# Attention on one Trainium2 core: four probability blocks of a chunk joined by three chained accumulating DMAs, row sums in two TensorE passes

## What is computed

```python
qkv = jnp.einsum('bnd,ed->bne', x, w_qkv)
q, k, v = jnp.split(qkv, 3, axis=-1)          # each to 16 heads of 32
dots = jnp.einsum('bhnd,bhmd->bhnm', q, k) * SCALE
attn = jax.nn.softmax(dots, axis=-1)
out = jnp.einsum('bhnm,bhmd->bhnd', attn, v)
```

## Time and profile before

| | us |
|---|---|
| median of three runs | 1830.68 |
| profiled execution, span from the first to the last instruction | 1825.5 |
| what lies between the two | 5.2 |
| busy: TensorE matmul | 1787.7 (98%) |
| busy: VectorE | 1455.1 (80%) |
| busy: ScalarE | 1448.1 (79%) |
| busy: POOL | 182.8 (10%) |
| VectorE adds into dve_sum, line 896, x320 of 2306 ns | 737.8 |
| DMA queue of POOL, share of 16 engines | 19.8% |

### The profile page before, as it was taken

One profiled execution on the slowest core, in us unless ns is written; L12 is line 12 of the kernel. 1 busy time (PEld: TensorE's weight loads), 2 busy tenths in 40 slices (PEclk: granted clock), 3 DMA queues, 4 the chain that ended last, 5 costly groups with the idle time before them and its releaser, 6 DMA issues. The chain is left out here.

```text
span 1825.5 us, 40458 instructions
## 1 busy us (share of the span) xinstructions
PE 1787.7 (98%) x16186; PEld 906.5 (50%) x16186; DVE 1455.1 (80%) x1582; ACT 1448.1 (79%) x1581; POOL 182.8 (10%) x158
## 2 busy tenths in 40 slices
PE   9999998999999999999999999999989999999997
PEld 7887885333333333333333333333336776644443
DVE  5444346889899898898998989989984778788898
ACT  5344357999999999999999999999965555556487
POOL 0000000010010010010010010100113221000044
PEclk9999999999999999999999999999999999999998
DMA  8665555436446346355464463464456440122075
GB/s 300 216 226 205 206 201 180 105 87 166 96 99 170 93 101 166 82 134 133 94 142 124 94 164 91 108 160 96 102 140 215 139 138 24 64 127 127 1 295 206
DMA packets 106370, 256.32 MB, mean 140 GB/s; under 512 B 8180, under 2 KB 24692, under 8 KB 96756
## 3 DMA queue, kind: packets, MB, share of 16 engines
q1 hardware_dynamic: 97012, 187.08, 28.5%
q0 software_dynamic: 9216, 67.11, 19.8%
HBM read 105.01 MB, written 82.05 MB: 102 GB/s over the span
## 5 line engine op out<-in xcount | busy, mean ns | idle before, releaser
L896 DVE TENSOR_TENSOR dve_sum<-dve_sum,probs 128x2048 f32<-128x2048 f32 x320 | 737.8, 2306 | 13.1 <-ACT probs L817 3.3
L817 ACT ACTIVATE probs<-score_others,shift_now 128x1536 f32<-128x1536 f32 x384 | 597.5, 1556 | 0.0
L984 PE MATMUL mixed_ps<-probs,value_piece 128*32 128x512 f32 (+1 forms) x3840 | 407.9, 515 | 1.2 <-ACT probs L817 0.2
L816 ACT ACTIVATE probs<-score_first,shift_now 128x512 f32<-128x512 f32 x384 | 266.5, 694 | 4.1 <-PE score_others L951 1.1
L951 PE MATMUL score_first<-first_queries,key_piece 32*128 32x512 f32 x768 | 245.4, 424 | 4.6 <-ACT probs L816 3.0
L951 PE MATMUL score_others<-first_queries,key_piece 32*128 32x512 f32 x2304 | 247.8, 425 | 0.0
L951 PE MATMUL score_others<-q_second,key_piece 32*128 32x512 f32 x2304 | 247.3, 424 | 0.0
L951 PE MATMUL score_first<-q_second,key_piece 32*128 32x512 f32 x768 | 245.1, 424 | 0.1
L951 PEld LDWEIGHTS score_first<-q_second,key_piece 32*128 32x128 f32 x768 | 122.0, 183 | 183.6 <-ACT probs L816 100.8
L951 PEld LDWEIGHTS score_first<-first_queries,key_piece 32*128 32x128 f32 x768 | 121.8, 183 | 183.2 <-ACT probs L816 84.3
L817 ACT ACTIVATE probs_paired<-score_others,shift_now 128x1536 f32<-128x1536 f32 x128 | 198.2, 1548 | 0.0
(11 more groups left out here) (252 smaller groups left out, 2596.7 us busy)
## 6 DMA issues: line engine op xcount, KB each, us to landing
probs_paired<-probs_paired POOLq DMA_DIRECT2D x64, 1024.0 KB, 8.0
o_scratch<-out_parts SPq DMA_DIRECT2D x33, 512.0 KB, 2.8
k_scratch<-parts SPq DMA_DIRECT2D x32, 512.0 KB, 4.9
q_scratch<-parts SPq DMA_DIRECT2D x32, 512.0 KB, 2.7
key_piece<-k_scratch SPq DMA_DIRECT2D x32, 512.0 KB, 5.2
h_scratch<-h SPq DMA_DIRECT2D x5, 2816.0 KB, 8.1
h<-h_scratch SPq DMA_DIRECT2D x5, 2816.0 KB, 11.4
v_scratch<-values SPq DMA_DIRECT2D x32, 256.0 KB, 2.0
```

Of the source, the lines that this page charges most:

```text
L816: nc.scalar.activation(block_probs(k)[:, 0:CH], score_first[:], ACT.Exp, bias=shift[:, c:c + 1], scale=SCALE).then_inc(probs_done, 1)
L817: nc.scalar.activation(block_probs(k)[:, CH:HPG * CH], score_others[n % 2][:], ACT.Exp, bias=shift[:, c:c + 1], scale=SCALE).then_inc(prob ...
L896: nc.vector.tensor_tensor(total[:], first[:], block_probs(k)[:], ALU.add).then_inc(dve_added, 1)
L984: last = nc.tensor.matmul(mixed_ps[j * HD:(j + 1) * HD, lo:hi], v_group[k // KPP][:, k % KPP, j * HD:(j + 1) * HD], block_probs(k)[:, j * ...
```

## The change

PAIRS becomes (2, 3) and (4, 5). Each pair's DMA waits for the values of its first block and the exponentials of its second, no longer for the values of the second. When both have landed, POOL issues a third DMA that adds the tile of blocks 2 and 3 to that of blocks 4 and 5. Two sum passes are left: one in step 0 from the joined tile, one in step 1 from dve_sum. VectorE adds the blocks 0, 1 and 6 to 15. ScalarE's waits for the four tiles are new: block 2 for the third DMA of the chunk before (four_landed, which POOL passes on), blocks 3 and 5 for its pair DMAs (pairs_landed), block 4 for the sums. Singles still share six tiles.

```diff
-    PAIRS = ((4, 5), (9, 10))
-    TO_SUMS = (0, 1)
+    PAIRS = ((2, 3), (4, 5))
     ADD_ORDER = [k for k in range(KB) if not any(k in pair for pair in PAIRS)]
 
-    SUMS_AT = ((0,), (1, 2))
+    SUM_PARTS = 2
+    SUMS_AT = ((0,), (1,))
...
-                            if i in TO_SUMS:
+                            if i is not None and k == PAIRS[i][1]:
+                                act.wait_ge(pairs_landed, it * CPB + c + 1)
+                            elif i == 0:
+                                act.wait_ge(four_landed, it * CPB + c + 1)
+                            elif i == 1:
                                 act.wait_ge(sums_done, it * CPB + c + 2)
-                            elif i is not None:
-                                act.wait_ge(dve_added, (it * CPB + c) * ADDS + added_at(PAIRS[i][0]))
...
-                            if pair_of(k) is None:
-                                v.wait_ge(probs_done, (it + 1) * EXPS + (c * KB + k + 1) * 2)
-                            else:
-                                v.wait_ge(joined[pair_of(k)], 16 * (it * CPB + c + 1))
+                            v.wait_ge(probs_done, (it + 1) * EXPS + (c * KB + k + 1) * 2)
...
+                pool.sem_inc(pairs_landed, 1)
+                pool.sem_inc(four_landed, 1)
                 pool.wait_ge(w_in, 16)
                 with pool.Fori(0, ITERS) as it:
                     for c in range(CPB):
                         for i, pair in enumerate(PAIRS):
 
-                            pool.wait_ge(mixed_done, (it + 1) * BLOCKS + c * KB + pair[1] + 1)
+                            pool.wait_ge(mixed_done, (it + 1) * BLOCKS + c * KB + pair[0] + 1)
+                            pool.wait_ge(probs_done, (it + 1) * EXPS + (c * KB + pair[1] + 1) * 2)
                             pool.sem_inc(may_join, 1)
-                            nc.gpsimd.dma_start(probs_paired[i][0][:], probs_paired[i][1][:], accum_op=ALU.add).then_inc(joined[i], 16)
+                            nc.gpsimd.dma_start(probs_paired[i][0][:], probs_paired[i][1][:], accum_op=ALU.add).then_inc(pair_joined, 16)
+                        pool.wait_ge(pair_joined, 16 * len(PAIRS) * (it * CPB + c + 1))
+                        pool.sem_inc(pairs_landed, 1)
+                        nc.gpsimd.dma_start(probs_paired[1][0][:], probs_paired[0][0][:], accum_op=ALU.add).then_inc(four_joined, 16)
                         if c == W_AT:
...
-                for signal in joined:
-                    pool.wait_ge(signal, 16 * ITERS * CPB)
+                        pool.wait_ge(four_joined, 16 * (it * CPB + c + 1))
+                        pool.sem_inc(four_landed, 1)
...
-                    if at < len(TO_SUMS):
-                        part = probs_paired[TO_SUMS[at]][0]
-                        pe.wait_ge(joined[TO_SUMS[at]], 16 * f)
+                    if at == 0:
+                        part = probs_paired[1][0]
+                        pe.wait_ge(four_joined, 16 * f)
                     else:
                         part = dve_sum[(f + 1) % 2]
                         pe.wait_ge(dve_added, (f + 1) * ADDS)
```

More of the change, by code:

```diff
@@ L698, in attend @@
         dve_added, may_join = sem("dve_added"), sem("may_join")
-        joined = [sem(f"joined{i}") for i in range(len(PAIRS))]
+        pair_joined, four_joined = sem("pair_joined"), sem("four_joined")
+        pairs_landed, four_landed = sem("pairs_landed"), sem("four_landed")
         mixed_copied = sem("mixed_copied")
@@ L971, in sums @@
                         last = nc.tensor.matmul(mixed_ps[j * HD:(j + 1) * HD, :], keep.ones[:, 0:HD], part[:, j * CH:(j + 1) * CH],
-                                                start=at == 0, stop=at == len(TO_SUMS))
-                    if at == len(TO_SUMS):
+                                                start=at == 0, stop=at == SUM_PARTS - 1)
+                    if at == SUM_PARTS - 1:
                         last.then_inc(sums_done, 1)
@@ L1015, in first_product @@
                                          start=m == 0, stop=m == len(terms) - 1)
-                for at in range(len(TO_SUMS) + 1):
+                for at in range(SUM_PARTS):
                     sums(CHUNKS, at)
```

## The result

The changed kernel takes 1863.43 us, the median of four runs (1861.02 to 1866.18), against 1830.84 us before: a ratio of 1.0174, with a 95% interval of 1.0155 to 1.0193. It is slower by 32.6 us. (A ratio and its interval are estimated from the fast runs of both kernels, and can differ by up to 0.002 from the quotient of the two medians.) The forecast was 8 us faster, and the range ended at 1843.

The account below looks back on a forecast made before the run. TensorE was taken to lead, with 1.3 us of ScalarE's slack. Span 1825.5 - 19 (removed pass) + 11 (late chain in seven loading chunks) = 1817.5; from the median, 1830.7 - 8 = 1822.5 us, range 1810 to 1843.

Parts of the forecast that it names:

- the signs that it set for being wrong: Quiet chunks waiting for the DMA, seven loading chunks below 33 or above 37 us, or last-values copy late behind VectorE's adds.
- What bounds the kernel: Attention chunks of 33.2 us: TensorE's contiguous steps add up to 33.1 us and lead, with 1.3 us of ScalarE's slack behind.
- The removed pass: Step 1, one sum pass fewer: 0.6 us a chunk gained, 0.3 turned into a wait for VectorE; 19 us over 32 chunks.
- VectorE's stop before block 6: VectorE's adds in each chunk: 0.4 to 0.5 us idle before block 6, covered by 0.4 us spare, costed at nothing.
- Rival C: VectorE becomes the bound: its last add comes 0.3 us later, quiet gain 10 us, chain loses 8, about 1829 us; chance 0.17.
- The quiet chain: Three DMAs in chunks without loads: landing at 624.6, needed by 626.5, 2 us to spare; 24 or 25 chunks keep 0.6.
- Rival A: The three-DMA chain is on time everywhere, in loading chunks too: 1811.5 us; chance 0.22.
- The loading chain: Three DMAs in seven chunks that fetch keys and values: landed at 562.3, needed at 560.2, 2.1 us late.
- The loss per late chunk: Step 0 after a loading chunk: 2.1 us late, 0.4 comes back, loss 1.6 us x 7 = 11 us.
- The last chunk: End of attention: other loads in it and no next chunk to hold up, so no lateness counted.
- rival B: Step 0 after the loading chunks: chain late by much more, 4.4 x 7 = 31 us lost, 1842.5 us; chance 0.28.
- The rule against the trace: GpSimd-issued 1 MB DMA: the skill's fit gives 4.4 us, the trace 6.9 to 10.5; by the fit the chain is never late.

Follow-up runs that it names:

- less_pass: The kernel before with the second of its three sum passes left out, DMAs, loads and waits as before: 1814.92 us, ratio 0.9908.
- stall_half_filled: The changed kernel with 18 idle matmuls ahead of step 0's wait for the third DMA in the chunks after loads: 1849.47 us, ratio 1.0110.
- nothing_beside_end: The changed kernel, loading chunks fetching only the first keys early, other loads and store after the third DMA; last chunk's output and token loads also held: 1897.32 us.
- third_skipped: The changed kernel with the third DMA adding only 128 of 2048 columns in the fourth chunk of each iteration: 1816.72 us, ratio 0.9922.
- keys_ahead3: The changed kernel, loading chunks fetching first and second keys ahead of the DMA chain, first values beside it, the rest and the store after: 1841.80 us, ratio 1.0055.
- loads_after: The changed kernel, loading chunks storing early and issuing the second to fourth load pieces only after the third DMA has landed: 1857.71 us, ratio 1.0138.

## Why the prediction was wrong

Point by point, by its own steps. Of the signs that it set for being wrong two came: the seven chunks took above 37 us (38.27 to 39.05), and four quiet chunks show the wait for the chain, though of 1.08 us at most. Two slips in its sums are small: 2.1 less 0.4 is 1.7 and not 1.6, and 1830.7 - 8 is 1822.7.

*What bounds the kernel*, right: TensorE leads, with ScalarE close behind, and less_pass shows it.

*The removed pass*, right in kind, 0.52 us a chunk for 0.6. The waits for dve_sum and for the last values stayed small, and VectorE's stop before block 6 is there and covered, as costed:

```profile
680.88 20.90 DVE L896 TENSOR_TENSOR dve_sum<-dve_sum,probs 128x2048 f32<-128x2048 f32 x9 [0.52 <-ACT probs L820]
702.18 0.69 DVE L831 COPY mixed<-mixed_ps 128x512 f32<-128x512 f32 x1 [0.40 <-PE mixed_ps L990]
```

VectorE idles 0.52 us ahead of block 6, where 0.4 to 0.5 was foreseen, and still waits 0.40 us for the last values, which is the spare that was worked out. Rival C is out.

*The quiet chain*, right in that it costs almost nothing, wrong in its size: the third DMA is issued 14.05 us after the first in the chunk at 614.79 (12.7 to 14.3 in all 24), for 12.5 predicted, since a second DMA behind the first lands 6.5 us after it (3.8 + 9.7 - 7.0) and not 5.0. The 5.0 was meant as the later of two bounds, and the measured landing lies beyond it. Of the 2 us of spare next to nothing was left: hence the four short waits. Rival A, the chain in time everywhere, is out by that alone.

*The loading chain* is the step that failed, and in it one term: "5.0 + 1.1 for the second behind it". By that the second lands 6.1 us behind the first and 14.2 us after the first is issued; measured were 8.2 to 9.6 us and 16.6 to 17.9 (17.5 in the chunk at 680.13, 3.9 + 13.6). About half of the miss, 1.5 us, is not the loads at all: it is the 6.5 for 5.0 that quiet chunks show too. The other half is that the loads delay the landing of the second by some 4 us (13.5 us after the first is issued in a quiet chunk, 17.5 here), where the forecast has 2.2 (1.1 for each of the two). I took that slowing from a DMA with no other accumulating DMA beside it (8.1 for 7.0) and used it for one queued behind another. The third DMA, 9.8 us by forecast, took 9.3 to 10.1, and the first 8.3 to 8.4 for 8.1. So the chain was not 2.1 but 5.0 us late: landing at 707.5, needed by the forecast's rule at 701.96 + 0.5. Over the seven it was 4.8 to 5.5 us late.

*The loss per late chunk* was taken as lateness less 0.4. There the clock was missing: 1.4 to 1.5 us, shown by stall_half_filled. 5.0 - 0.4 + 1.5 = 6.1 beside the 5.9 that a loading chunk takes above a quiet one.

*The last chunk* was costed at nothing because no chunk comes after it. Its sums do, and they wait longest of all, and at the lower clock:

```profile
1389.64 1.94 PE L977 MATMUL mixed_ps<-probs_paired,ones 128*32 128x512 f32 x8 [6.59 <-DMA probs_paired<-probs_paired]
```

The output and token loads beside the chain do there what the key loads do elsewhere (10.4, 12.1 and 10.1 us for its three DMAs); nothing_beside_end shows it, where they are held back and the three take 7.6, 9.7 and 7.4 us. What it costs is known less well: from the last chunk's first DMA to the end of the span it is 497.3 us, and 491.5 in third_skipped, where TensorE waits for that DMA 2.9 us at most. In the other runs with this end unchanged and the full third DMA the stretch takes 495.0 to 501.0 us, so the end costs some 4 to 9 us.

The sum with the measured terms: 1830.8 - 24 x 0.52 + 7 x 5.4 = 1856, and some 6 for the end make 1862. Of the 41 us between forecast and result some 20 are the chain's lateness (2.9 us for seven chunks), 10 the clock, 6 the end, and 2 or 3 the dearer pass. The outcome was rival B, at the place and by the mechanism named, with its price too low: 41 us (7 x 5.9) for 31 in the chunks above their quiet time, and the end on top. *The rule against the trace*, the 4.4 us for 1 MB by the Trainium skill (DMA: Bandwidth & Descriptors, "Anatomy of one DMA — SWDGE (gpsimd) path"), was no help: no run shows less than 6.9 us for an accumulating DMA of 1 MB.

What stays open: why a second accumulating DMA lands 6.5 us behind the first even with no loads beside it, why 768 KB of loads beside it cost it a further 2.4 to 3.6 us, and why more loads beside it cost hardly more. The runs show the sizes and that it is the loads; how the engines share their time was not looked into.

## What to carry to other kernels

A chain of dependent DMAs adds up its latencies, and each link depends on what else is then on the engines: price the slowest place of its loop, not the median. Don't price a DMA that is queued behind another from one that ran without such a neighbour: here the loads delayed the first by 1.3 us and the landing of the second by 4. Where a chain pays in most places and is late in a few, leave it out in the few. And a wait of TensorE can cost more than its length: here 4.7 us of waiting cost 1.4 to 1.5 us more, in slow matmuls behind it.

## What the runs showed of the hardware that I had not expected

- Two accumulating 1 MB DMAs issued 3.8 us apart land 6.5 us apart, though with no other one in flight each lands 7.0 to 8.0 us after its issue in most quiet chunks of the kernel before: the second took 9.7 us (after, quiet chunk at 614.79; 8.4 to 10.4 in all 24). Beside loads of 768 KB it took 12.1 to 13.3 (keys_ahead3), beside 768 KB and a store 13.7 to 14.6 (loads_after).
- After 4.7 us of waiting TensorE ran at a mean granted clock of 0.57 over the next 4 us, mostly at 1.2 and not 2.4 GHz, and the passes to step 2 took 4.42 us instead of 2.91. 18 idle matmuls in the wait kept the clock at 1.00.
